# Softmax in a cross-attention kernel: eight exponentials with bias and accumulator on ScalarE in place of one wide exponential and two VectorE passes

## The chip, the cores and the metric

The kernel runs on one core of one Trainium2 chip. The metric is the device time of one execution in microseconds. The profile is that of one further execution of the same program.

## The reference, cut to what matters

Sixteen batches of 1024 tokens, 512 wide, go through a cross-attention over 64 context rows with 8 heads, and then through a mixture of 32 experts (4 per token, 512 places each) with one shared expert beside it. Both parts add to their input.

```python
x = x + xattn(layernorm(x), ctx, Wq, Wk, Wv, Wo, bo)   # q, k, v in 8 heads of 64
    scores = einsum('bhid,bhjd->bhij', q, k) * scale    # 8 heads x 64 columns for each token
    attn = softmax(scores, axis=-1)
    out = einsum('bhij,bhjd->bhid', attn, v)
x = x + ffn(layernorm(x), gate_w, bias, W1, W3, W2, sw1, sw3, sw2)
```

## The kernel before, in words

The program has two parts, one after the other: `set_up_and_tokens` and `experts`. The change lies in the first, which takes some 1440 of the 2031 us of the profile.

The first part takes the tokens in 128 tiles of 128 tokens. A tile passes through many stages, and a loop over steps runs them against each other: step n does the scores of tile n-8 (`SCORES`), the mixing of the values for tile n-9 (`MIX`), the second layernorm and its transposes for tile n-14 (`X2`), and so on. Every fourth step belongs to a group of four tiles, for the shared expert: two steps of each period of four do its upward products (`FFN_UP`, into the banks G_ps and U_ps), the other two the downward ones (`FFN_DOWN`). Below, a tile is named by the number of its scores. Tiles 62, 63, 66 and 67 fall into steps with upward products (tile 62 and 66 the first of the two, 63 and 67 the second), tiles 64 and 65 into steps with downward ones, and so with every other period. In every second period, the step of the last tile (75, for one) also makes keys or values of a later batch (`kv`, evicted by ScalarE into `kbd` or `vbd`); tile 63's and 67's do not.

Each engine has one queue, written out by hand in the order of `step(n)`, and waits with semaphores. No scheduler moves anything. The path of a tile's softmax crosses four engines:

- TensorE (PE): 12 matmuls of the scores into the bank S_ps (L350), and behind them in its queue the mixing of the tile before (L366), gate logits, the transposes of x2 (L376), the shared expert's products, a piece of preparation for the next batch (PREP_ps), and last the four transposes of this tile's probabilities into TP_ps (L477).
- VectorE (DVE): the maximum of each head, into `top_s` (L902); the subtraction of it from S_ps, in place (L915); after the exponential the sums of each head (L934) and their reciprocal `rsum` (L943).
- ScalarE (ACT): one exponential of 128x512 with the layernorm's `rs1` as per-token scale (L576). Ahead of it in the queue stands `x2` (L567), behind it `x2t_h` (L584), in the up steps the `Tanh` of the shared expert (L610, waits for G_ps) and, when VectorE has multiplied it twice (L749, L754), `ht_h` (L613). The next step begins with `pt_h` (L542), the high half of the turned probabilities.
- GpSimd (POOL): the product of the exponentials with `rsum` (L655). Ahead of it in the queue stand `ht_l` (L642, waits for `ht_h`, in the step after an up step), `xt_l` (L649), and four indirect DMAs of the slot table (L631).

The scores of the next tile stand right behind the transposes L477 in TensorE's queue.

## Time and profile before

| what | value |
|---|---|
| median of 3 runs | 2043.02 us (2042.87 to 2050.21) |
| the profiled execution, its own time | 2032.71 us |
| its span in the profile | 2030.9 us |
| TensorE busy | 1805.0 us, 89% |
| VectorE busy | 1511.0 us, 74% |
| ScalarE busy | 736.6 us, 36% |
| GpSimd busy | 1227.6 us, 60% |

The span runs from the first to the last instruction; the 1.8 us around it belong to the execution's own time. The profiled execution was 10.3 us faster than the median. Busy shares are means over both parts of the program, which have different limits, so the stretches have to be read apart.

### The profile page before, as it was taken

What the parts mean: (1) busy time and instruction counts of PE and PEld (TensorE: products, weight loads), DVE (VectorE), ACT (ScalarE), POOL (GpSimd) and SP (SyncE); (2) the same over time, 40 slices, a digit from 0 to 9 for tenths busy, and PEclk for the clock granted to TensorE, in tenths of its full rate; (3) what the DMA queues carried; (4) which work ended last, traced back from release to release, by engine and by line L of the source; (5) the groups of instructions that cost most, each with busy time, mean ns of one, the idle gap of its engine ahead of it and who ended that gap; (6) DMA issues with size and microseconds to landing.
All of it is one profiled execution on the core that took longest, in us unless ns stands there. A gap on an engine that the chain in (4) does not pass through costs nothing. (4 is left out here: it accounts for less than half of the span.)

```text
span 2030.9 us, 31738 instructions
## 1 busy us (share of the span) xinstructions
PE 1805.0 (89%) x9952; PEld 1281.4 (63%) x9952; DVE 1511.0 (74%) x4072; ACT 736.6 (36%) x1252; POOL 1227.6 (60%) x1107
## 2 busy tenths in 40 slices
PE   5789799999999999999999999999750899999992
PEld 4667577777777777777777777776420456555551
DVE  4678688898798889888889888888540477766671
ACT  2233334334434333434333343333210344444440
POOL 1223556666566666566666666666465487888864
PEclk8999899999999999999999999999885899999996
DMA  6123453343233333323323323332214599999986
GB/s 199 54 72 85 79 102 102 95 100 115 88 104 101 96 95 112 94 86 119 96 87 103 113 85 97 105 96 79 67 60 127 148 228 220 231 227 228 228 153 80
DMA packets 194903, 241.43 MB, mean 119 GB/s; under 512 B 59569, under 2 KB 101809, under 8 KB 194738
## 3 DMA queue, kind: packets, MB, share of 16 engines
q1 hardware_dynamic: 149682, 169.89, 28.8%
q0 software_dynamic: 45056, 69.52, 17.3%
q8 instruction: 82, 1.34, 0.3%
q14 instruction: 83, 0.68, 0.1%
HBM read 134.07 MB, written 105.25 MB: 118 GB/s over the span
## 5 line engine op out<-in xcount | busy, mean ns | idle before, releaser
L631 POOL DMA_INDIRECT slot_table<-tok,slot x512 | 504.1, 985 | 128.1 <-issue 122.8
L649 POOL TENSOR_TENSOR xt_l<-xt,xt_h 128x512 fp32r<-128x512 f32 x128 | 165.4, 1293 | 165.8 <-PE S_ps L350 130.3
L1102 POOL DMA_INDIRECT out<-ye,idx x128 | 202.5, 1582 | 89.2 <-issue 35.8
L655 POOL TENSOR_TENSOR prob<-prob,rsum 128x512 f32<-128x512 f32 x128 | 133.8, 1045 | 154.1 <-DVE rsum L943 153.6
L576 ACT ACTIVATE prob<-S_ps,rs 128x512 f32<-128x512 f32 x128 | 88.0, 688 | 364.9 <-DVE S_ps L915 364.9
L1254 DVE TENSOR_TENSOR xe_l<-TE_ps,xe_h 128x512 f16<-128x512 f32 x128 | 88.5, 692 | 177.0 <-issue 90.6
L350 PE MATMUL S_ps<-a_h,xt_h 128*128 128x512 f32 x512 | 214.2, 418 | 1.8 <-DVE m_l L878 1.8
L642 POOL TENSOR_TENSOR ht_l<-hid,ht_h 128x512 fp32r<-128x512 f32 x64 | 83.1, 1298 | 204.7 <-ACT ht_h L613 204.7
L366 PE MATMUL O_ps<-m_h,pt_h 128*128 128x512 f32 x512 | 200.8, 392 | 2.7 <-ACT pt_h L542 2.2
L350 PE MATMUL S_ps<-a_h,xt_l 128*128 128x512 f32 x512 | 202.7, 396 | 0.0
L350 PE MATMUL S_ps<-a_l,xt_h 128*128 128x512 f32 x512 | 201.4, 393 | 0.0
L366 PE MATMUL O_ps<-m_l,pt_h 128*128 128x512 f32 x512 | 199.9, 390 | 0.0
L366 PE MATMUL O_ps<-m_h,pt_l 128*128 128x512 f32 x512 | 199.8, 390 | 0.0
L873 DVE TENSOR_TENSOR pt_l<-TP_ps,pt_h 128x512 fp32r<-128x512 f32 x128 | 88.4, 690 | 118.5 <-ACT pt_h L542 113.3
L1090 POOL DMA_INDIRECT rows<-x2aug,idx x128 | 133.7, 1045 | 43.5 <-issue 38.1
L542 ACT ACTIVATE pt_h<-TP_ps 128x512 fp32r<-128x512 f32 x128 | 75.5, 590 | 204.6 <-PE TP_ps L477 200.5
L1154 PE MATMUL TE_ps<-ident_r,rows 128*128 128x128 f32 x512 | 70.4, 263 | 76.7 <-DMA rows<-x2aug,idx 65.3
L477 PE MATMUL TP_ps<-ident,prob 128*128 128x128 f32 x512 | 81.7, 283 | 50.5 <-POOL prob L655 50.5
L1154 PEld LDWEIGHTS TE_ps<-ident_r,rows 128*128 128x128 f32 x512 | 58.0, 144 | 102.7 <-issue 62.0
L567 ACT ACTIVATE x<-xr,nb,rs 128x512 f32<-128x512 f32 x128 | 104.1, 813 | 42.6 <-DMA x2aug<-x 32.5
L477 PEld LDWEIGHTS TP_ps<-ident,prob 128*128 128x128 f32 x512 | 58.5, 142 | 92.2 <-POOL prob L655 62.1
L366 PEld LDWEIGHTS O_ps<-m_h,pt_h 128*128 128x128 f32 x512 | 96.5, 188 | 26.8 <-issue 2.7
(177 smaller groups left out, 4889.7 us busy)
## 6 DMA issues: line engine op xcount, KB each, us to landing
xt<-in_xT SPq DMA_DIRECT2D x128, 256.0 KB
xr<-in_x SPq DMA_DIRECT2D x32, 1024.0 KB, 6.1
x2aug<-x SPq DMA_DIRECT2D x128, 256.0 KB
out<-xr SPq DMA_DIRECT2D x32, 1024.0 KB
up_w<-in_w SPq DMA_DIRECT2D x64, 256.0 KB
slot_table<-tok,slot POOLq DMA_INDIRECT x512
down_raw<-in_w SPq DMA_DIRECT2D x32, 256.0 KB
x2aug<-wfull SPq DMA_DIRECT2D x32, 64.0 KB
```

Source lines behind the costliest of these rows:

```text
L350: last = pe.matmul(S_ps[:, :], left[:, kc, :], right[:, b % 2, kc, :], start=(m == 0), stop=(m == 3 * KD - 1))
L366: last = pe.matmul(O_ps[:, :], left[:, p * P:(p + 1) * P], right[:, b % 2, p, :], start=(m == 0), stop=(m == 3 * PAIRS - 1))
L477: last = pe.transpose(TP_ps[:, p * P:(p + 1) * P], prob[:, t % 2, 2 * p:2 * p + 2, :].rearrange("p h j -> p (h j)"), ident[:, :])
L567: act.activation(x2[:, :], x_tile(t), ACT.Identity, bias=nb2[:, g % 2, i:i + 1], scale=rs2[:, g % 2, i:i + 1]).then_inc(x2_done, 1)
L631: pool.indirect_dma_start(table, bass.IndirectOffsetOnAxis(ap=slot[:, g % 2, i, q:q + 1], axis=0), tok[:, t:t + 1], None, bounds_check=SLO ...
L649: pool.tensor_tensor(xt_l[:, :, :], xt[:, :, :], xt_h[:, t % 2, :, :].bitcast(F32), ALU.subtract).then_inc(xt_lo, 1)
L655: pool.tensor_tensor(prob[:, t % 2, :, :], prob[:, t % 2, :, :], rsum[:, :].unsqueeze(2).to_broadcast([P, H, SKV]), ALU.mult).then_inc(pro ...
L873: dve.tensor_tensor(pt_l[:, :], TP_ps[:, :], pt_h[:, :].bitcast(F32), ALU.subtract).then_inc(pt_lo, 1)
L1090: pool.indirect_dma_start(rows[:, r, c, :].bitcast(F32), None, x2aug, bass.IndirectOffsetOnAxis(ap=idx[:, e, c:c + 1], axis=0), bounds_che ...
L1102: pool.indirect_dma_start(out, bass.IndirectOffsetOnAxis(ap=idx[:, e, c:c + 1], axis=0), ye[:, e % 4, c, :], None, bounds_check=TOKENS + P ...
L1154: last = pe.transpose(TE_ps[i % 2][:, kc * P:(kc + 1) * P].bitcast(F32R), rows[:, e % RING, i, kc * P:(kc + 1) * P], ident_r[:, :])
L1254: dve.tensor_tensor(xe_l[dst], TE_ps[i % 2][:, :].rearrange("p (c t) -> p c t", c=KD), xe_h[dst], ALU.subtract).then_inc(t_lo, 1)
```

## The change

VectorE no longer subtracts the maximum from the scores and no longer sums the exponentials. It makes a small tile `below` of 128x8 instead, which holds minus the maximum times `rs1`. ScalarE takes the exponential of each head by itself, with that head's column of `below` as bias, `rs1` as scale, and the sum of the head's 64 results written through the accumulator output into `sums`. One signal is given, after the eighth. The wait for `ln1` moves from ScalarE to VectorE; ScalarE gets a wait for `rsum_done` of the tile before, and VectorE one for `exp_done` of the tile before. `below` has two buffers.

```diff
@@ ACT, step(n) @@
                         act.wait_ge(below_done, t + 1)
-                        act.wait_ge(ln1, (g + 1) * NEWTON)
                         after(act, probs_t_done, t - 1)
-                        act.activation(prob[:, t % 2, :, :], S_ps[:, :].rearrange("p (h j) -> p h j", h=H), ACT.Exp,
-                                       scale=rs1[:, g % 2, i:i + 1]).then_inc(exp_done, 1)
+                        after(act, rsum_done, t)
+                        for h in range(H):
+                            last = act.activation(prob[:, t % 2, h, :], S_ps[:, h * SKV:(h + 1) * SKV], ACT.Exp,
+                                                  bias=below[:, t % 2, h:h + 1], scale=rs1[:, g % 2, i:i + 1],
+                                                  accum_out=sums[:, h:h + 1])
+                        last.then_inc(exp_done, 1)
@@ DVE, step(n) @@
                         dve.wait_ge(max_done, s8 + 1)
-                        dve.tensor_tensor(heads, heads, top_s[:, :].unsqueeze(2).to_broadcast([P, H, SKV]),
-                                          ALU.subtract).then_inc(below_done, 1)
+                        dve.wait_ge(ln1, (s8 // 4 + 1) * NEWTON)
+                        after(dve, exp_done, s8 - 1)
+                        dve.tensor_scalar(below[:, s8 % 2, :], top_s[:, :], rs1[:, s8 // 4 % 2, s8 % 4:s8 % 4 + 1], -1.0,
+                                          ALU.mult, ALU.mult).then_inc(below_done, 1)
@@
-                    if s8 is not None:
-                        dve.wait_ge(exp_done, s8 + 1)
-                        dve.tensor_reduce(sums[:, :], prob[:, s8 % 2, :, :], AX.X, ALU.add).then_inc(sum_done, 1)
@@
                     if s8 is not None:
-                        dve.wait_ge(sum_done, s8 + 1)
+                        dve.wait_ge(exp_done, s8 + 1)
                         after(dve, prob_done, s8)
                         dve.reciprocal(rsum[:, :], sums[:, :]).then_inc(rsum_done, 1)
```

On ScalarE, in the last up step of a period without keys and the start of the step after it, the queue reads before (L584 is `x2t_h`, L610 the `Tanh` of G_ps, L613 `ht_h`, L542 the next step's `pt_h`):

```order
L559 ACTIVATE xt_h<-xt 128x512
L567 ACTIVATE x2<-xr,nb2,rs2 128x512
L576 ACTIVATE prob<-S_ps,rs1 128x512
L584 ACTIVATE x2t_h<-TX_ps 128x4x128
L610 ACTIVATE hid<-G_ps 128x512
L613 ACTIVATE ht_h<-hid 128x512
L542 ACTIVATE pt_h<-TP_ps 128x512
```

and now:

```order
L560 ACTIVATE xt_h<-xt 128x512
L568 ACTIVATE x2<-xr,nb2,rs2 128x512
L578 ACTIVATE prob,sums<-S_ps,below,rs1 128x64 x8
L588 ACTIVATE x2t_h<-TX_ps 128x4x128
L614 ACTIVATE hid<-G_ps 128x512
L617 ACTIVATE ht_h<-hid 128x512
L543 ACTIVATE pt_h<-TP_ps 128x512
```

One instruction became eight in the same place; what stands behind it kept its order.

On VectorE, in the step behind that one (tile 64's), from the maximum to the reciprocal, before:

```order
L902 TENSOR_REDUCE top_s<-S_ps 128x8
L915 TENSOR_TENSOR S_ps<-S_ps,top_s 128x512
L930 TENSOR_TENSOR xr<-xr,O_ps 128x512
L934 TENSOR_REDUCE sums<-prob 128x8
L939 BN_STATS st2<-xr 128x6
L943 RECIPROCAL rsum<-sums 128x8
```

and now:

```order
L906 TENSOR_REDUCE top_s<-S_ps 128x8
L921 TENSOR_SCALAR below<-top_s,rs1 128x8
L936 TENSOR_TENSOR xr<-xr,O_ps 128x512
L942 BN_STATS st2<-xr 128x6
L946 RECIPROCAL rsum<-sums 128x8
```

The two passes over 128x512 are gone, and the reciprocal stands right behind L942, waiting for ScalarE.

## Rows read from the trace of the kernel before

**Rows 1.** Busy time by engine in a stretch; then PEclk, DMA share, GB/s

```profile
700.00:1000.00 300.00, 294.65 (x1686) 221.06 (x1685) 260.43 (x780) 118.42 (x206) 192.79 (x181) 1.00 0.33 98
```

**Rows 2.** Waits: engine, line, releaser; us in total, times, longest

```profile
PE TP_ps L477 <- POOL prob L655: 50.5, 39, 9.4
```

**Rows 3.** Groups of ScalarE: count, busy us, mean ns, idle before

```profile
L567 ACT ACTIVATE x<-xr,nb,rs 128x512 f32<-128x512 f32 x128 | 104.1, 813 | 42.6 <-DMA x2aug<-x 32.5 <-issue 7.5 <-DVE nb L727 2.6
L576 ACT ACTIVATE prob<-S_ps,rs 128x512 f32<-128x512 f32 x128 | 88.0, 688 | 364.9 <-DVE S_ps L915 364.9
L559 ACT ACTIVATE xt_h<-xt 128x512 fp32r<-128x512 f32 x128 | 80.9, 632 | 12.4 <-DMA xt<-in_xT 12.4
...
L542 ACT ACTIVATE pt_h<-TP_ps 128x512 fp32r<-128x512 f32 x128 | 75.5, 590 | 204.6 <-PE TP_ps L477 200.5 <-issue 4.1
...
L604 ACT ACTIVATE lexp<-R_ps 128x128 f32<-128x128 f32 x32 | 8.7, 272 | 6.5 <-remote 6.5
```

**Rows 4.** Groups of VectorE, with the same columns

```profile
L915 DVE TENSOR_TENSOR S_ps<-S_ps,top_s 128x512 f32<-128x512 f32 x128 | 87.5, 684 | 1.2
...
L934 DVE TENSOR_REDUCE sums<-prob 128x8 f32<-128x512 f32 x128 | 86.9, 679 | 23.6 <-ACT prob L576 21.8 <-issue 1.8
...
L794 DVE MATCH_VALUE_LOAD taken<-best,biased 128x8 f32 x128 | 10.4, 82 | 0.3 <-DVE best L787 0.3
```

**Rows 5.** Timeline of ScalarE, tiles 62, 63: start, duration, idle before and releaser

```profile
725.80 0.69 ACT L576 ACTIVATE prob<-S_ps,rs 128x512 f32<-128x512 f32 x1 [2.47 <-DVE S_ps L915]
...
728.89 0.60 ACT L610 ACTIVATE hid<-G_ps 128x512 f32<-128x512 f32 x1 [0.75 <-PE G_ps L402]
...
738.22 0.69 ACT L576 ACTIVATE prob<-S_ps,rs 128x512 f32<-128x512 f32 x1 [3.81 <-DVE S_ps L915]
...
739.83 0.60 ACT L610 ACTIVATE hid<-G_ps 128x512 f32<-128x512 f32 x1 [0.43 <-PE G_ps L402]
```

**Rows 6.** The same of ScalarE, tiles 66 and 75 (keys are made beside 75)

```profile
768.74 0.69 ACT L576 ACTIVATE prob<-S_ps,rs 128x512 f32<-128x512 f32 x1 [2.85 <-DVE S_ps L915]
...
771.23 0.60 ACT L610 ACTIVATE hid<-G_ps 128x512 f32<-128x512 f32 x1 [0.80 <-PE G_ps L402]
...
868.02 0.69 ACT L576 ACTIVATE prob<-S_ps,rs 128x512 f32<-128x512 f32 x1 [3.81 <-DVE S_ps L915]
868.61 0.59 ACT L584 ACTIVATE x2t_h<-TX_ps 128x512 f16<-128x512 f32 x1
870.60 1.20 ACT L596 ACTIVATE vbd<-PREP_ps 64x512 f32<-64x512 f32 x2 [1.40 <-PE PREP_ps L439]
872.33 0.60 ACT L610 ACTIVATE hid<-G_ps 128x512 f32<-128x512 f32 x1 [0.53 <-PE G_ps L402]
```

**Rows 7.** Timeline of VectorE: last product of tile 63's step; two of tile 65's

```profile
742.68 0.66 DVE L754 TENSOR_TENSOR hid<-hid,U_ps 128x512 f32<-128x512 f32 x1
...
758.39 0.67 DVE L915 TENSOR_TENSOR S_ps<-S_ps,top_s 128x512 f32<-128x512 f32 x1
...
761.24 0.18 DVE L943 RECIPROCAL rsum<-sums 128x8 f32<-128x8 f32 x1
```

**Rows 8.** Timeline of GpSimd: tile 61's product; then tile 64's step

```profile
718.57 1.04 POOL L655 TENSOR_TENSOR prob<-prob,rsum 128x512 f32<-128x512 f32 x1 [1.52 <-DVE rsum L943]
...
744.09 1.30 POOL L642 TENSOR_TENSOR ht_l<-hid,ht_h 128x512 fp32r<-128x512 f32 x1 [2.46 <-ACT ht_h L613]
...
751.60 1.06 POOL L655 TENSOR_TENSOR prob<-prob,rsum 128x512 f32<-128x512 f32 x1
```

**Rows 9.** Timeline of TensorE: transposes of tiles 61, 64, 65 and 66

```profile
720.33 0.66 PE L477 MATMUL TP_ps<-ident,prob 128*128 128x128 f32 x4
...
752.72 0.66 PE L477 MATMUL TP_ps<-ident,prob 128*128 128x128 f32 x4 [0.97 <-POOL prob L655]
...
762.60 0.66 PE L477 MATMUL TP_ps<-ident,prob 128*128 128x128 f32 x4
...
773.64 0.60 PE L477 MATMUL TP_ps<-ident,prob 128*128 128x128 f32 x4
```

More of the change, by code:

```diff
@@ L150, in set_up_and_tokens @@
         top_s = sb("top_s", [P, H], F32)
+        below = sb("below", [P, 2, H], F32)
         sums = sb("sums", [P, H], F32)
@@ L216, in set_up_and_tokens @@
         x2_t_done, logits_done = sem("x2_t_done"), sem("logits_done")
-        max_done, below_done, sum_done, rsum_done = sem("max_done"), sem("below_done"), sem("sum_done"), sem("rsum_done")
+        max_done, below_done, rsum_done = sem("max_done"), sem("below_done"), sem("rsum_done")
         exp_done, pt_hi, x2_done, x2t_hi = sem("exp_done"), sem("pt_hi"), sem("x2_done"), sem("x2t_hi")
```

## The prediction

> **What bounds the kernel now.** I read first the busy times by stretch, because the two parts of the program differ. In the middle of the part with tokens TensorE is busy 294.7 us of 300, at the full clock (1.00, so 2.4 GHz), VectorE 260.4, ScalarE only 118.4 [rows 1]. TensorE's queue sets the pace, and any wait that reaches it is paid in full. Next the waits: TensorE stood 50.5 us, 39 times, before the transposes of the probabilities, for GpSimd's product with the reciprocal [rows 2]. The end of the softmax path is thus already what TensorE waits for. Last the timelines, for who makes it late. For tile 64 the wait is 0.97 us [rows 9]; the product there started at 751.60 without idle time in front [rows 8], so GpSimd's own queue was the limit: from `ht_l` at 744.09 to this product are 7.51 us of queued work, and `ht_l` had waited for `ht_h` [rows 8], which waits for VectorE's last product at 742.68 [rows 7], which goes back to the Tanh of tile 63 at 739.83 [rows 5]. For tile 65 there is next to no spare: the reciprocal began at 761.24 [rows 7], and the transposes at 762.60 [rows 9]. VectorE and ScalarE have idle time on average, which is worth nothing unless it lies on one of these two paths.
>
> **What goes.** Per tile VectorE loses the subtraction, 684 ns, and the sums, 679 ns [rows 4], and gains `below`, 128x8, which I price as the reciprocal of the same shape, 0.18 us [rows 7]: 1.18 us less, 151 us of busy time over 128 tiles. Little of it shortens the path, since the reciprocal now waits for ScalarE.
>
> **What comes, E.** I call E the time from the start of the first of eight exponentials to the end of the eighth. One exponential of 512 columns is 688 ns now. A copy of 512 columns from PSUM takes 590, an exponential of 128 columns with a fixed scale 272, so a column costs (590-272)/384 = 0.83 ns and 64 columns 272-53 = 219 ns. Two operands read per partition (bias and scale) cost 813-632 = 181 ns more. That makes 400 ns for one head [rows 3]. Neighbours on ScalarE overlap by 0.1 us: tile 75's exponential takes 0.69 us from 868.02, and `x2t_h` begins at 868.61 [rows 6]. So 0.30 us apart, and E = 8 x 0.30 + 0.10 = 2.5 us if the accumulator's output is free. No row shows an accumulator output. The nearest is VectorE's match, one call in the program that leaves an extra row of 82 ns [rows 4]; on ScalarE the fixed part of the shortest ACTIVATE, 272-106 = 166 ns [rows 3], is what a second, tiny instruction per head could take. Overlapped it adds 0.07 and E is 3.1; not overlapped it adds 0.17 and E is 3.8; if it also takes away the overlap of its neighbours, 8 x 0.566 = 4.5. I take the middle, 3.4, and keep 2.5 and 4.5 as ends. E below 2.5 would need deeper overlap than these rows have.
>
> The page "ScalarE: Activation LUTs" of the Trainium skill (section "What ACT_TABLE_LOAD costs") gives 280 ns + 0.833 ns per column with a pointer bias, 93 ns for each further pointer and an overlap of 93 ns. By it E would be 8 x 0.333 + 0.09 = 2.8 without the accumulator, and the sum below about +25 us. The trace agrees on the pointer (688 against 590 ns, [rows 3]). The page's budget of 0.3 us per ACTIVATE speaks against splitting one into eight. "VectorE: DVE Perf Modes" (section "Two Vector instructions with no wait between them") says that on VectorE an accumulator output is a second instruction; no row here shows it for ScalarE.
>
> **The softmax path itself.** Before, the subtraction began 2.85 us ahead of the reciprocal in tile 65 (758.39, 761.24) [rows 7]. Now: `below` 0.17 + hand-over 0.05 + E + hand-over 0.04 = E + 0.26 (the hand-overs are estimates from starts and ends of neighbouring engines' rows). With E = 3.4 that is 3.66: +0.81 us. Tile 65 has nothing to spare, so TensorE pays 0.8. Tile 61, the same place in another period, ends its product at 718.57 + 1.04 = 719.61, and TensorE comes at 720.33 [rows 8, 9]: it pays 0.14. Half the 32 periods are of each kind: 16 x 0.81 + 16 x 0.14 = 15 us. Tile 66, in an up step, pays nothing: its exponentials end at 771.64 (below), and with 0.04 and the 1.36 us from reciprocal to transposes (761.24 to 762.60) its probabilities are ready at 773.04, before TensorE comes at 773.64 [rows 9].
>
> **What is queued behind the exponentials.** In the up steps the Tanh stands behind `x2t_h`, and in the first of them also behind `lexp`. The exponential starts 0.5 us earlier than now (0.22 behind the start of the small operation, against 0.67 + 0.05 behind the subtraction's). Tile 66: 768.24, end 771.64, Tanh 0.56 later at 772.20 instead of 771.23, +0.97. Tile 62: 725.30, end 728.70, Tanh 729.26 instead of 728.89, +0.38 [rows 5, 6]. From there it goes through both VectorE products, `ht_h`, `pt_h`, to the next maximum, all one after the other: the next tile starts that much later, less where TensorE's own delay covers it. Tile 63 (with tile 66's or tile 62's delay, by kind): exponentials 737.72 to 741.12, Tanh 0.39 later at 741.51 instead of 739.83, +1.68, and with the delay carried in +2.65 or +2.06. GpSimd cannot start `ht_l` before that has passed, and its 7.51 us follow unchanged. The reciprocal of tile 64 arrives another 0.18 us later than this queue. TensorE, which had waited 0.97 already, pays it all: 2.83 or 2.24, mean 2.53. In it lies what tile 63's own transposes lose. In periods with keys ScalarE first has to wait 1.40 us for the keys and 0.53 for G_ps [rows 6]; tile 75's exponentials run 867.52 to 870.92, the eviction follows at 871.31 instead of 870.60 and the Tanh at 872.5: +0.2, with the carried delay and the 0.18 from 0.7 to 1.3, mean 1.0. Sum: 16 x 2.53 + 16 x 1.0 = 56 us.
>
> **The sum.** 15 + 56 = 71 us in the part with tokens; the part with experts has none of these instructions. On the profiled execution 2032.7 + 71 = 2104 us; the median of runs lies 10 us higher, so 2043 + 71 = 2114 us, +3.5%. By the same steps E = 2.5 gives +13 us, 3.1 +41, 3.8 +124, and 4.5 +221: above 3 each 0.1 us of E costs about 10 us or more, since delays pass from one step to the next.
>
> **Rivals.** (a) *The accumulator is free*, E = 2.5: 2056 us. For it: the program has one instruction per head. Against it: 8 results must be written somewhere. (b) *Each head is fully serial*, E = 4.5: 2264 us. For it: a read of the accumulator has to wait for its ACTIVATE. Against: the 0.1 us overlap everywhere else. (c) *Faster*: the short ACTIVATEs overlap far more than wide ones, down to E = 1.7 or less; then the Tanh of tile 63 still waits only for G_ps (738.22-0.5+1.7+0.39 = 739.81, [rows 5]), no queue behind is late, and VectorE's lighter load of memory accesses lets GpSimd's six operations ahead of tile 64's product run 0.1 us shorter each: 32 x 0.6 = 19 us less, 2024 us. It decides below E = 1.7, against 400 ns each from [rows 3]. (d) *VectorE's relief cancels the cost*: its 1.18 us per tile would pull the maxima forward. Against it: VectorE waits at the start of most steps for `pt_h` anyway. It would give 2035 to 2050.
>
> **Chances.** Forecast with E from 2.8 to 4.1: 60%. (a) 14%, (b) 15%, (c) 4%, (d) 7%. The range takes in (a) and most of (b): 2050 to 2230 us. A measurement of this kernel tells about 0.5% (10 us) from no change: faster 5%, same 9%, slower 86%.
>
> **What would show it.** In the changed profile: E itself, from eight rows of ScalarE, and whether rows of an accumulator's read stand between; VectorE's busy time down by about 150 us, with new idle time before the reciprocal, released by ScalarE; the idle time of ScalarE before Tanh gone in up steps; TensorE's wait for GpSimd before L477 grown from 50 to about 120 us; the distance `ht_l` to product in tile 64 still 7.5 us. I am wrong if E is under 2 or over 4.5, if TensorE's clock falls with its waits, or if tile 64's product starts from VectorE's reciprocal long after its own queue was free.

## The result, and the profile after

| | before | after |
|---|---|---|
| median | 2044.8 us (2042.87 to 2050.21, 4 runs) | 2146.55 us (2140.51 to 2154.34, 4 runs) |
| profiled execution, its own time | 2032.71 us | 2154.34 us |
| span | 2030.9 us | 2152.6 us |

The kernel is slower: ratio 1.0501 [1.0469, 1.0532], +102 us, where 71 had been forecast. The two profiled executions lie further apart, 121.7 us, since that of before was 12 us under its median and that of after 8 us over its own. The busy times of the page, first the whole program after (engine, us, share, instructions), then its costliest groups of the softmax path:

```profile
PE 1852.4 (86%) x9952; PEld 1306.2 (61%) x9952; DVE 1438.8 (67%) x3944; ACT 1043.5 (48%) x3172; POOL 1226.1 (57%) x1107
...
L578 ACT ACTIVATE prob<-S_ps,below,rs 128x64 f32<-128x64 f32 x1024 | 398.0, 409 | 376.3 <-DVE below L921 373.2
...
L578 ACT ACTIVATION_READ_ACCUMULATOR prob<-S_ps,below,rs 128x1 f32 x1024 | 214.6, 210 | 0.0
...
L946 DVE RECIPROCAL rsum<-sums 128x8 f32<-128x8 f32 x128 | 25.9, 203 | 208.9 <-ACT prob L578 208.1
```

VectorE is busy 72 us less (1511.0 to 1438.8) although two passes of 87.5 and 86.9 us are gone [rows 4], ScalarE 307 us more. There is an instruction that the kernel does not write out: behind each of the 1024 exponentials stands a read of the accumulator, 210 ns by itself. The reciprocal now stands idle for ScalarE for 208 us.

Most of the time is in the middle of the tokens' part. A stretch from the first score matmul of tile 20 to that of tile 124, 104 tiles, of before and then of after (columns as in [rows 1]):

```profile
257.60:1397.80 1140.20, 1115.35 (x6376) 834.55 (x6375) 979.51 (x2931) 447.52 (x776) 720.31 (x676) 1.00 0.34 99
```

```profile
275.80:1512.10 1236.30, 1151.41 (x6377) 850.17 (x6375) 924.72 (x2827) 696.61 (x2336) 718.42 (x676) 0.98 0.32 91
```

104 tiles take 96.1 us longer; of the rest of the 121.7 us, 18.2 lie ahead of this stretch (it begins at 275.80 instead of 257.60) and 7.4 behind it. TensorE's idle time in the stretch went from 24.9 to 84.9 us (length less busy time), and its busy time rose by 36 us for the same matmuls: the granted clock is 0.98 instead of 1.00. So there are two losses, waits and a slower clock. The waits, and the answers to [rows 1] and [rows 2]:

```profile
700.00:1000.00 300.00, 281.43 (x1554) 206.95 (x1552) 222.26 (x686) 170.15 (x571) 173.50 (x164) 0.98 0.32 93
```

```profile
PE TP_ps L478 <- POOL prob L659: 112.8, 69, 12.9
...
ACT hid L614 <- PE G_ps L403: 6.6, 7, 2.6
```

TensorE waits 112.8 us for GpSimd's product (50.5 before). The idle time of ScalarE before the Tanh, for TensorE's G_ps, is nearly gone: 6.6 us in the whole program, 39.8 before.

**Tile 64 of the kernel after**, engine by engine. ScalarE, which answers to [rows 5, 6] (start, duration; idle time before and its releaser):

```profile
797.40 0.62 ACT L588 ACTIVATE x2t_h<-TX_ps 128x512 f16<-128x512 f32 x1
797.87 0.63 ACT L614 ACTIVATE hid<-G_ps 128x512 f32<-128x512 f32 x1
...
806.84 0.40 ACT L578 ACTIVATE prob<-S_ps,below,rs 128x64 f32<-128x64 f32 x1 [2.98 <-DVE below L921]
807.15 0.19 ACT L578 ACTIVATION_READ_ACCUMULATOR prob<-S_ps,below,rs 128x1 f32 x1
807.24 0.39 ACT L578 ACTIVATE prob<-S_ps,below,rs 128x64 f32<-128x64 f32 x1
...
809.82 0.22 ACT L578 ACTIVATION_READ_ACCUMULATOR prob<-S_ps,below,rs 128x1 f32 x1
```

The first two rows are of tile 63's step: the Tanh stands right behind `x2t_h`, without idle time. The others give E = 809.82 + 0.22 - 806.84 = 3.20 us. An exponential takes 0.40, its read starts 0.09 before its end, and the next exponential 0.09 behind the start of the read: 0.38 us per head by (809.53 - 806.84)/7.

VectorE, tiles 63 and 64, which answers to [rows 7]:

```profile
794.07 0.23 DVE L921 TENSOR_SCALAR below<-top_s,rs 128x8 f32<-128x8 f32 x1
...
804.78 0.68 DVE L906 TENSOR_REDUCE top_s<-S_ps 128x8 f32<-128x512 f32 x1
805.50 1.31 DVE L921 TENSOR_SCALAR below<-top_s,rs 128x8 f32<-128x8 f32 x1
...
810.07 0.20 DVE L946 RECIPROCAL rsum<-sums 128x8 f32<-128x8 f32 x1 [1.95 <-ACT prob L578]
```

The same operation on 128x8 numbers takes 0.23 us in one tile and 1.31 in the next. It is so in nearly every period: in 25 of the 26 tiles of tile 64's place in the stretch it takes over 0.7 us, with a mean of 1.28 over the 26, and in the other three places at most 0.32. GpSimd in the same step, which answers to [rows 8]:

```profile
801.75 1.28 POOL L646 TENSOR_TENSOR ht_l<-hid,ht_h 128x512 fp32r<-128x512 f32 x1 [2.85 <-ACT ht_h L617]
...
805.47 1.30 POOL L653 TENSOR_TENSOR xt_l<-xt,xt_h 128x512 fp32r<-128x512 f32 x1
...
810.36 1.04 POOL L659 TENSOR_TENSOR prob<-prob,rsum 128x512 f32<-128x512 f32 x1 [1.16 <-DVE rsum L946]
```

`xt_l` started 0.03 us before `below` and ended at 806.77; `below` ended at 806.81. The product waited 1.16 us for the reciprocal: its own queue was free at 809.20, 7.45 us behind `ht_l`, nearly the 7.51 of before.

TensorE, which answers to [rows 9]:

```profile
811.46 0.72 PE L478 MATMUL TP_ps<-ident,prob 128*128 128x128 f32 x4 [2.05 <-POOL prob L659]
...
812.40 0.63 PE L351 MATMUL S_ps<-a_l,xt_h 128*128 128x512 f32 x1
...
816.07 0.39 PE L351 MATMUL S_ps<-a_h,xt_l 128*128 128x512 f32 x1
```

and the granted clock in three stretches of scores, tiles 64, 65 and 66 (the column before the DMA share):

```profile
799.30:802.40 3.10, 3.05 (x15) 2.21 (x13) 2.18 (x12) 1.36 (x3) 0.66 (x1) 1.00 0.69 247
811.80:816.10 4.30, 4.30 (x15) 3.44 (x14) 3.06 (x9) 2.30 (x4) 1.72 (x2) 0.60 0.01 0
824.10:827.20 3.10, 3.10 (x17) 2.51 (x16) 3.07 (x10) 2.42 (x4) 1.67 (x2) 1.00 0.11 36
```

TensorE had stood idle 2.05 us; in the stretch behind it the clock is 0.60 on average, which is 1.2 GHz for most of it, and a score matmul takes 0.63 us instead of 0.39. From the start of the first of a tile's 12 score matmuls to the start of the last are 2.6 us at full clock. It took over 3 us in 16 of the 104 tiles, always behind a tile of tile 64's place in its period; before, in one. I call these slow scores.

### The profile page after: what moved, and what is told of

It reads as the page before. It is cut to its first block and busy times, and to the rows that moved or that the text cites. A ratio compares the mean times of both kernels' runs of the same rounds, so it can differ in the third digit from the quotient of the medians.

```text
span 2152.6 us, 33657 instructions
## 1 busy us (share of the span) xinstructions
PE 1852.4 (86%) x9952; PEld 1306.2 (61%) x9952; DVE 1438.8 (67%) x3944; ACT 1043.5 (48%) x3172; POOL 1226.1 (57%) x1107
## 5 line engine op out<-in xcount | busy, mean ns | idle before, releaser
L578 ACT ACTIVATE prob<-S_ps,below,rs 128x64 f32<-128x64 f32 x1024 | 398.0, 409 | 376.3 <-DVE below L921 373.2
L351 PE MATMUL S_ps<-a_h,xt_h 128*128 128x512 f32 x512 | 226.8, 443 | 1.8 <-DVE m_l L882 1.8
L578 ACT ACTIVATION_READ_ACCUMULATOR prob<-S_ps,below,rs 128x1 f32 x1024 | 214.6, 210 | 0.0
L351 PE MATMUL S_ps<-a_l,xt_h 128*128 128x512 f32 x512 | 213.3, 417 | 0.0
L351 PE MATMUL S_ps<-a_h,xt_l 128*128 128x512 f32 x512 | 212.7, 415 | 0.0
L478 PE MATMUL TP_ps<-ident,prob 128*128 128x128 f32 x512 | 85.3, 291 | 112.8 <-POOL prob L659 112.8
L946 DVE RECIPROCAL rsum<-sums 128x8 f32<-128x8 f32 x128 | 25.9, 203 | 208.9 <-ACT prob L578 208.1
```

What stands on the lines that cost most here:

```text
L351: last = pe.matmul(S_ps[:, :], left[:, kc, :], right[:, b % 2, kc, :], start=(m == 0), stop=(m == 3 * KD - 1))
L478: last = pe.transpose(TP_ps[:, p * P:(p + 1) * P], prob[:, t % 2, 2 * p:2 * p + 2, :].rearrange("p h j -> p (h j)"), ident[:, :])
L578: last = act.activation(prob[:, t % 2, h, :], S_ps[:, h * SKV:(h + 1) * SKV], ACT.Exp, bias=below[:, t % 2, h:h + 1], scale=rs1[:, g % 2, ...
```

## Steps per place in the period

For the experiments I use one table, worked out from the starts of the first score matmul of each tile, tiles 20 to 123: the mean time from one tile to the next, in us, by the place in the period of four. "64" is tile 64's place, and so on. The last columns are the 104 tiles together and how many of them had slow scores.

```
kernel     "64"   "65"   "66"   "63"   104 tiles  slow scores
before     10.44  10.33  10.90  12.17  1140.2     1
after      12.30  11.57  10.95  12.73  1236.3    16
x_warm     12.25  10.72  10.93  12.70  1211.7     0
x_pos      11.92  10.33  10.94  12.20  1180.1     2
x_port     10.87  10.17  10.92  12.17  1147.1     0
x_read     12.28  11.67  10.91  12.84  1240.4    10
x_read2    12.07  10.90  11.38  12.71  1223.7     4
x_queue    11.22  10.33  10.97  12.26  1164.3     0
x_split    11.18  10.91  10.93  12.59  1185.7     1
x_same     10.41  10.31  10.98  12.18  1140.8     1
x_pool2     9.61  10.59  10.92  12.17  1125.6     0
x_onemax   10.49  10.16  10.90  12.14  1136.0     0
x_best      9.69  10.22  11.05  12.15  1120.8     0
```

A slow set of scores lengthens the step of the place "65" (11.57 in after, 10.72 where the clock holds). Single long steps are in the means too: in the profiles of before, x_same, x_onemax and x_best TensorE stood idle for 11 to 20 us between 200 and 310 us for ScalarE's `x2`, which waited for a DMA. They fall ahead of tile 20 or behind it, and 5 us there are 0.2 us in a mean of 26. The ratios below are each against the kernel before on the same chip; its median there was 2036.0 us (x_warm, x_pos, x_port, x_read), 2019.9 (x_queue, x_split, x_pool, x_best) and 2037.2 us (x_read2, x_same, x_pool2, x_onemax), so ratios, and not times, are compared.

## Experiments on the place and the neighbour of `below`

My theory after the trace: the eight exponentials cost what was forecast, and the surplus comes from `below`, which waits for GpSimd, and from the clock. The rival: ScalarE's longer work alone makes all of it.

**x_pos.** `below` right behind the maximum, instead of behind three chains of other work.

```diff
                         dve.tensor_reduce(top_s[:, :], heads, AX.X, ALU.max).then_inc(max_done, 1)
+                        dve.wait_ge(max_done, s8 + 1)
+                        dve.wait_ge(ln1, (s8 // 4 + 1) * NEWTON)
+                        after(dve, exp_done, s8 - 1)
+                        dve.tensor_scalar(below[:, s8 % 2, :], top_s[:, :], rs1[...], -1.0,
+                                          ALU.mult, ALU.mult).then_inc(below_done, 1)
                     chain(n, 2, 3)
...
                     chain(n, 3, 4)
-                    (the same lines, from here)
```

> The changed kernel, with VectorE's small operation that makes the bias placed directly behind the maximum, ahead of the statistics and Newton steps that stood between. It still runs on VectorE from SBUF operands. Theory: in tiles 62, 63, 65, 66 the exponentials start 0.6 to 1.6 us earlier, the Tanh of tile 63 with them, and tile 65's transposes no longer wait; in tile 64, where the operation stood right behind the maximum already, it keeps its 1.3 us (0.23 elsewhere), which it spends beside GpSimd's xt_l and so is a wait for GpSimd. Time 2080 to 2100 us. Rival (the place does not matter, since ScalarE is late by itself): above 2135.

Measured: 2089.16 us, ratio 1.0253 [1.0198, 1.0308]. Half of the loss is gone with the eight exponentials, the reads and E = 3.2 us untouched. In tile 65's place the cost is gone entirely (10.33). In tile 64's place it is not. VectorE of x_pos, tile 64, and its group over the whole program:

```profile
772.63 1.31 DVE L910 TENSOR_SCALAR below<-top_s,rs 128x8 f32<-128x8 f32 x1
```

```profile
L910 DVE TENSOR_SCALAR below<-top_s,rs 128x8 f32<-128x8 f32 x128 | 116.0, 906 | 4.5
```

Beside it, GpSimd of x_pos:

```profile
772.61 1.30 POOL L653 TENSOR_TENSOR xt_l<-xt,xt_h 128x512 fp32r<-128x512 f32 x1
```

Again it starts within 0.02 us of `xt_l` and ends with it. The mean of `below` rose to 906 ns from 485 in the kernel after, since at the new place it meets GpSimd's work in more tiles; the steps of the other places are at most 0.04 us longer than before. What `below` had stood behind was partly such a wait itself: in tile 63 of the kernel after, a Newton step of 1.69 us, shown further below.

**x_port.** The bias by ScalarE itself: the maximum is negated in its reduction, and a ninth, small ACTIVATE multiplies it by `rs1`. VectorE's small operation is gone, all else is as after.

```diff
-                        dve.tensor_reduce(top_s[:, :], heads, AX.X, ALU.max).then_inc(max_done, 1)
+                        after(dve, below_done, s8)
+                        dve.tensor_reduce(top_s[:, :], heads, AX.X, ALU.max, negate=True).then_inc(max_done, 1)
...
+                        act.wait_ge(max_done, t + 1)
+                        act.wait_ge(ln1, (g + 1) * NEWTON)
+                        act.activation(below[:, t % 2, :], top_s[:, :], ACT.Identity,
+                                       scale=rs1[:, g % 2, i:i + 1]).then_inc(below_done, 1)
                         act.wait_ge(below_done, t + 1)
...
-                        (VectorE's tensor_scalar into below, with its waits)
```

> The changed kernel, with the bias made by ScalarE itself (one ACTIVATE of 128x8 with rs1 as scale, on a maximum that VectorE's reduction already negates); VectorE's small operation is gone. It differs from x_pos by the engine. Theory (in tile 64 VectorE's small operation waited 1.1 us for GpSimd): exponentials of tile 64 start 1.0 us earlier than in x_pos, TensorE's idle time there falls under 1 us and the clock does not drop in tile 65: 2050 to 2075 us. Rival (the 1.3 us of the small operation is work and not a wait): within 10 us of x_pos, since ScalarE gives 0.3 us for it.

Measured: 2048.87 us, ratio 1.0066 [1.0046, 1.0087], 1 us under the range's lower end. ScalarE and GpSimd of x_port, tile 64:

```profile
767.40 0.30 ACT L576 ACTIVATE below<-top_s,rs 128x8 f32<-128x8 f32 x1 [1.24 <-issue]
767.73 0.40 ACT L582 ACTIVATE prob<-S_ps,below,rs 128x64 f32<-128x64 f32 x1
```

```profile
767.39 1.29 POOL L657 TENSOR_TENSOR xt_l<-xt,xt_h 128x512 fp32r<-128x512 f32 x1
```

The small operation starts 0.01 us behind the same GpSimd instruction and takes 0.30 us. So GpSimd's work delays it on VectorE and not on ScalarE. Between x_pos and x_port the 104 tiles differ by 33.0 us; 26 tiles of tile 64's place by 1.31 - 0.30 = 1.0 us are 26, and the two slow sets of scores of x_pos are some 4 more. E is 3.21 us here too: ScalarE does all that it does in the change and one ACTIVATE more, and the kernel costs 0.7%. The rival falls.

The page "SBUF — State Buffer" of the Trainium skill (section "SBUF: two separate sides") says that VectorE, in its faster modes or with two inputs in this memory, and GpSimd share a pair of ports to it, that whichever starts first holds it for its whole instruction, and that ScalarE has its own. The trace agrees for `below` in tile 64, though which mode VectorE was in no row tells: it ended 0.04 us behind `xt_l`, which had started first. On who starts first other rows do not bear the page out: the Newton step of 1.69 us began 0.36 us ahead of `xt_l`, and still ended 0.04 behind it; a DMA of the slot table stood on GpSimd until just before, but beside such a DMA alone the same step took 0.15 us (1391.19 in the kernel before). VectorE's pass over PSUM was not delayed. The subtraction, at the same place in the kernel before, took 684 ns on average over 128 [rows 4], and in tile 64 it ran beside the same GpSimd instruction:

```profile
747.84 1.30 POOL L649 TENSOR_TENSOR xt_l<-xt,xt_h 128x512 fp32r<-128x512 f32 x1
747.85 0.70 DVE L915 TENSOR_TENSOR S_ps<-S_ps,top_s 128x512 f32<-128x512 f32 x1
```

## Experiment on the clock

**x_warm.** The kernel after, with eight matmuls that nobody reads put ahead of the wait for the probabilities in tile 64's place of each period. They fill TensorE's idle time there and change nothing else.

```diff
-                    pe.wait_ge(prob_done, t + 1)
...
+                    if t % 4 == 0 and t >= 8:
+                        for k in range(8):
+                            pe.matmul(TP_ps[:, :], ones[:, :], up_sb[:, 0, :], start=True, stop=True)
+                    pe.wait_ge(prob_done, t + 1)
```

> The changed kernel, with eight matmuls of 128x512 that nobody reads, written into TP_ps ahead of TensorE's wait for the probabilities in every fourth step (tiles 64, 68, ...), from tile 8 on. They take about 1.8 of the 2.05 us in which TensorE stands idle there. Theory (the idle time of tile 64 lets the granted clock fall, and the scores of tile 65 then run at half rate: 4.0 instead of 2.6 us in the changed kernel's trace): the scores of tile 65 take 2.6 us again, PEclk 1.00 in the middle stretch, and some 17 to 21 drops of 1.5 us each go: 2113 to 2123 us. Rival (the slow scores have another cause, such as reads of memory beside them): unchanged at 2146 or slower.

Measured: 2122.24 us, ratio 1.0423 [1.0383, 1.0463]. No tile has slow scores, and the 104 tiles take 1211.7 us instead of 1236.3, at a granted clock of 1.00:

```profile
270.80:1482.50 1211.70, 1167.84 (x6560) 851.83 (x6584) 921.32 (x2833) 697.34 (x2336) 719.16 (x676) 1.00 0.32 93
```

Nearly all of the 24.6 us lies in the place "65" (11.57 to 10.72, 26 x 0.85 = 22 us); the steps of tile 64's place, with their wait for the probabilities, stayed as long (12.30 and 12.25). So the clock cost about 25 us in the stretch, beside the idle time ahead of it, and the remaining +71.5 us are waits.

## Experiments on the exponentials and the accumulator

**x_read.** The kernel after without `accum_out`: VectorE sums again, with the second layernorm's statistics between sums and reciprocal.

```diff
-                                                  bias=below[...], scale=rs1[...], accum_out=sums[:, h:h + 1])
+                                                  bias=below[...], scale=rs1[...])
...
+                        dve.tensor_reduce(sums[:, :], prob[:, s8 % 2, :, :], AX.X, ALU.add).then_inc(sum_done, 1)
                         (bn_stats of the tile before)
+                        dve.wait_ge(sum_done, s8 + 1)
                         dve.reciprocal(rsum[:, :], sums[:, :]).then_inc(rsum_done, 1)
```

> The changed kernel, with the exponentials written without the accumulator output and the sums made by VectorE again (one pass of 128x512, 0.68 us, behind the eighth exponential). Everything else as changed. Theory (what is queued behind the exponentials on ScalarE carries the cost): the read of the accumulator, 0.09 us apart per head in the changed kernel, goes, E falls from 3.2 to 2.5 us, and the Tanh in up steps comes 0.7 us earlier; the softmax path itself stays about as long (0.75 us less, 0.65 us more for the sums). Time 2105 to 2125 us, from 2146. Rival (only the length of the softmax path counts): path within 0.1 us, time unchanged, 2140 to 2150.

Measured: 2156.9 us, ratio 1.0594 [1.0553, 1.0636]. I had expected less time than after, and it took more. E fell to 2.47 us, as it should, but the path from there to the reciprocal grew:

```profile
809.50 0.69 DVE L939 TENSOR_REDUCE sums<-prob 128x8 f32<-128x512 f32 x1 [1.95 <-ACT prob L578]
810.11 0.68 DVE L944 BATCH_NORM_STATS2 st<-xr 128x6 f32<-128x512 f32 x1
810.71 0.19 DVE L948 RECIPROCAL rsum<-sums 128x8 f32<-128x8 f32 x1
```

The reciprocal starts 1.21 us behind the first of them, not 0.6: the statistics stood in its way. From the first exponential to the reciprocal are 2.47 + 0.04 + 1.21 = 3.72 us, and 3.24 in the kernel after. I had counted the sums and not what was queued behind them.

**x_read2.** The same with the reciprocal right behind the sums.

```diff
                         dve.tensor_reduce(sums[:, :], prob[:, s8 % 2, :, :], AX.X, ALU.add).then_inc(sum_done, 1)
+                        dve.wait_ge(sum_done, s8 + 1)
+                        dve.reciprocal(rsum[:, :], sums[:, :]).then_inc(rsum_done, 1)
                         (bn_stats of the tile before)
-                        (the reciprocal, from here)
```

> x_read with VectorE's reciprocal directly behind the sums, ahead of the statistics of the second layernorm, which in x_read stood between and cost 0.6 us on the softmax path. So the softmax path is as long as in the changed kernel (0.73 us less of exponentials, 0.65 more of sums) and ScalarE's queue 0.73 us shorter. Theory (x_read was slow because of that order): ratio to the kernel before between 1.035 and 1.050, under the changed kernel's. Rival (the pass over prob costs more than its 0.65 us, through other operations that it pushes back): 1.055 or more, as x_read.

Measured: 2130.81 us, ratio 1.0449 [1.0409, 1.0489], as expected. From the end of the exponentials to the reciprocal are 0.75 us, and E is 2.48: together 3.23, as much as the 3.20 and 0.04 of the kernel after. So the accumulator is even on the path: eight reads add (3.20 - 2.48) = 0.72 us, 0.09 each, and save one pass of 0.7 us. What it wins beside that is VectorE's time, and in one place TensorE waits for it: in 24 of the 26 tiles of the place "66" the step of x_read2 takes some 0.3 us more. In tile 66 of both kernels VectorE goes without idle time into `pt_l`, the low half of the turned probabilities, which the mixing needs, and there it ends 0.33 us later in x_read2. (The interval of x_read2 overlaps that of the kernel after, [1.0469, 1.0532], it has 12 sets of slow scores fewer, and I don't read a gain into the difference.)

**x_split.** The kernel before, with its exponential as eight of 64 columns, the fixed `rs1` scale, no bias and no accumulator; subtraction and sums stay.

```diff
-                        act.activation(prob[:, t % 2, :, :], S_ps[:, :].rearrange(...), ACT.Exp, scale=rs1[...]).then_inc(exp_done, 1)
+                        for h in range(H):
+                            last = act.activation(prob[:, t % 2, h, :], S_ps[:, h * SKV:(h + 1) * SKV], ACT.Exp, scale=rs1[...])
+                        last.then_inc(exp_done, 1)
```

> The kernel before, with its exponential of 128x512 split by heads into eight of 128x64, with neither bias nor accumulator output; VectorE subtracts and sums as before. The cost of eight instructions alone: E = 8 x 0.21 + 0.1 = 1.8 us instead of 0.69. Theory (path and queue both get 1.1 us longer): tile 65 pays 1.1 or 0.4 us, tile 64 0.3 to 0.8 us: 30 to 50 us over the kernel before. Rival (GpSimd's queue covers it): under 10 us.

Measured: 2073.65 us, ratio 1.0264 [1.0229, 1.03], +53.8 us, a little over the range. Its group on ScalarE, and a row of its timeline:

```profile
L577 ACT ACTIVATE prob<-S_ps,rs 128x64 f32<-128x64 f32 x1024 | 223.9, 330 | 378.0 <-DVE S_ps L917 378.0
```

```profile
792.72 1.55 ACT L577 ACTIVATE prob<-S_ps,rs 128x64 f32<-128x64 f32 x7 [2.37 <-DVE S_ps L917]
```

In tile 64 seven of them stand in one row of 1.55 us: (1.55 - 0.33)/6 = 0.20 us apart though each takes 0.33. E is 1.75, 1.06 longer than one wide one. That alone costs 45 us in the 104 tiles, spread over the places "64", "65" and "63": one microsecond more of E, with everything else as before, costs nearly half of what the whole change does (96.1). By itself the split is dearer than x_port, which splits too but leaves out the subtraction and the sums.

**x_queue.** The kernel before, with 14 small copies that nobody reads behind the exponential in ScalarE's queue. They don't touch the softmax path, only what stands behind it.

```diff
                                        scale=rs1[:, g % 2, i:i + 1]).then_inc(exp_done, 1)
+                        for k in range(14):
+                            act.activation(idle[:, k, :], wo_sb[:, k % PAIRS, 0:64], ACT.Copy)
```

> The kernel before, with fourteen small copies of 128x64 on ScalarE behind the one wide exponential, to a tile that nobody reads: about 2.1 us more in ScalarE's queue, nothing more on the softmax path. Theory (ScalarE's queue carries part of the cost by itself, through the Tanh of tile 63, ht_h and the late start of tile 64): Tanh of tile 63 about 1.5 us later, half of the periods pay 1.5 us, the others 0.3: 25 to 35 us over the kernel before, and up to 55 if the longer idle time of TensorE lets its clock fall. Rival (only the softmax path and the late bias count): 0 to 8 us over the kernel before.

Measured: 2046.39 us, ratio 1.0131 [1.011, 1.0153], +26.5 us, as expected. ScalarE of x_queue, tile 64, and the group:

```profile
768.82 0.69 ACT L577 ACTIVATE prob<-S_ps,rs 128x512 f32<-128x512 f32 x1 [2.37 <-DVE S_ps L918]
769.40 2.14 ACT L580 ACTIVATE idle<-wo_sb 128x64 bf16<-128x64 f32 x14
771.45 0.57 ACT L587 ACTIVATE x2t_h<-TX_ps 128x512 f16<-128x512 f32 x1
```

and GpSimd in the same step:

```profile
764.33 1.28 POOL L645 TENSOR_TENSOR ht_l<-hid,ht_h 128x512 fp32r<-128x512 f32 x1 [3.53 <-ACT ht_h L616]
...
771.80 1.06 POOL L658 TENSOR_TENSOR prob<-prob,rsum 128x512 f32<-128x512 f32 x1
```

The place "64" grows by 0.8 us, where the forecast saw it: Tanh late, `ht_h` late, GpSimd's queue late. The product again starts without idle time in front, 7.47 us behind `ht_l`, and on average over the 26 tiles `ht_l` stands 0.85 us later in the step than before, and the product 0.79. The other places hardly change. So the second term of the forecast exists apart from the first.

## Experiments on the kernel before: what the path was waiting for

If GpSimd's queue is the limit in tile 64, an order that shortens it should gain, and the repeat of before should show how far two builds differ.

**x_same.** The kernel before, unchanged.

> The kernel before, unchanged, profiled beside the three others of this job, so that their stretches can be compared on one chip: the middle of the part with tokens (tiles 20 to 124), the stretch of tiles 16 to 20, the gap between the two parts, and the part with experts. The ratio to the kernel before is 1.000 within its interval, and the middle stretch takes 1140 us.

Measured: 2038.08 us, ratio 0.9999 [0.9984, 1.0015]; 104 tiles in 1140.8 us (1140.2 in the profile of before).

**x_pool** and **x_pool2**, one kernel measured twice: the last two DMAs of the slot table behind GpSimd's product instead of ahead of it.

```diff
-                    file(at(n, TABLE), 2, TOP)
                     (the product with rsum)
+                    file(at(n, TABLE), 2, TOP)
```

> The kernel before, with the last two of a step's four slot-table DMAs put behind the product with the reciprocal in GpSimd's queue, instead of ahead of it. Theory (in tile 64 the product waits for GpSimd's own queue, not for the reciprocal): it starts 0.8 us earlier there, TensorE's idle time before L477 falls from 50 to about 20 us: 15 to 28 us under the kernel before. Rival (the reciprocal is what comes last): no change, within 5 us.

> x_pool once more, beside the profile of the kernel before on the same chip. In x_pool's trace the middle stretch (tiles 20 to 124) was only 1 us shorter than before's: tile 64 gained 0.8 us, but the bias-free subtraction of tiles 61 and 65 came 0.7 us later. Theory (the gain of 18 us lies outside the middle stretch): ratio 0.985 to 0.995 again, with the middle stretch at 1139 us and the difference in the first 20 tiles or the gap between the parts. Rival (the first measurement was drift): ratio 0.998 or more.

Measured: 2002.03 us, ratio 0.9907 [0.9886, 0.9928], and 2024.11 us, ratio 0.9928 [0.9903, 0.9954]. The ratio came as expected both times, but I had expected the second profile to show its gain outside the 104 tiles, and that was wrong: they take 1125.6 us, 15.2 less than in x_same. The first profile (1139.3 us) had hidden it behind two long steps, of tiles 20 and 24, which took 13 us more than the others of their place. TensorE waited there 4.1 and 6.1 us for ScalarE's `x2`, and that for a DMA (ScalarE stood idle 6.53 and 8.68 us for it); why the DMA was late I did not find. GpSimd in tile 64 of x_pool2:

```profile
749.08 1.04 POOL L654 TENSOR_TENSOR prob<-prob,rsum 128x512 f32<-128x512 f32 x1 [1.60 <-DVE rsum L943]
```

The product now waits 1.60 us for VectorE and starts 0.8 us earlier in the step than before. The two DMAs had taken 2.5 us of the queue ahead of it (749.14 to 751.60 in the kernel before); only 0.8 came off, since VectorE's path was right behind. The place "65" pays back 0.3 us of the 0.8 (10.31 to 10.59).

**x_onemax.** The change with one maximum for the whole row instead of one per head: one bias of 128x1 by ScalarE, one wide exponential, sums on VectorE with the reciprocal right behind. The softmax is the same with any shift common to a head's columns; a head whose scores lie far below the largest of the row would lose digits, and no run here shows how far apart heads can lie before that matters.

```diff
-                        dve.tensor_reduce(top_s[:, :], heads, AX.X, ALU.max).then_inc(max_done, 1)
+                        dve.tensor_reduce(top_s[:, 0:1], S_ps[:, :], AX.X, ALU.max, negate=True).then_inc(max_done, 1)
...
-                        dve.tensor_tensor(heads, heads, top_s[...].to_broadcast([P, H, SKV]), ALU.subtract)
...
+                        act.activation(below[:, t % 2:t % 2 + 1], top_s[:, 0:1], ACT.Identity, scale=rs1[...])
-                        act.activation(prob[...], S_ps[...], ACT.Exp, scale=rs1[...])
+                        act.activation(prob[...], S_ps[...], ACT.Exp, bias=below[:, t % 2:t % 2 + 1], scale=rs1[...])
```

> x_best with GpSimd's order as in the kernel before: one maximum over 512 columns, bias made by ScalarE, one exponential of 128x512 with it, reciprocal right behind the sums. Theory (in tile 64 the product waits for GpSimd's queue, so a shorter softmax path gains nothing there by itself): ratio 0.993 to 1.000, with the middle stretch 0 to 8 us shorter, and the wait of 0.9 us in tile 64 still there. Rival (the path decides): 0.983 as x_best.

Measured: 2022.24 us, ratio 0.9916 [0.9886, 0.9946], slightly better than expected. The 104 tiles take only 4.2 us less than before; in tile 64 the product still stands behind the DMAs (it starts at the same 6.0 us behind the scores, though the reciprocal is there at 4.1). Another 10 us (against x_same) were won in the first 16 tiles, which I had not expected and did not take apart.

**x_best.** Both together.

> The kernel before with three edits: one maximum over all 512 columns of a token instead of one per head (softmax is the same for any shift), negated by the reduction; bias of 128x1 made by ScalarE; one exponential of 128x512 with that bias, so that VectorE's subtraction goes and its sums stay, with the reciprocal right behind them; and GpSimd's order of x_pool. Theory: softmax path about 1 us shorter than before in every step, ScalarE's queue 0.4 us longer, no wait of TensorE left before L477: 25 to 35 us under the kernel before. Rival (TensorE's own work bounds it already): within 8 us.

Measured: 1987.0 us, ratio 0.9833 [0.9813, 0.9854], 33 us faster than before, as expected, and about the sum of what each brings alone (0.9928 and 0.9916). ScalarE and GpSimd in tile 64, then the waits and a stretch as in [rows 1]:

```profile
746.36 0.29 ACT L576 ACTIVATE below<-top_s,rs 128x1 f32<-128x1 f32 x1 [1.41 <-DVE top_s L907]
746.69 0.78 ACT L580 ACTIVATE prob<-S_ps,below,rs 128x512 f32<-128x512 f32 x1
```

```profile
748.73 1.04 POOL L658 TENSOR_TENSOR prob<-prob,rsum 128x512 f32<-128x512 f32 x1 [1.08 <-DVE rsum L940]
```

```profile
PE TP_ps L478 <- POOL prob L658: 24.5, 12, 9.8
```

```profile
700.00:1000.00 300.00, 299.84 (x1717) 225.09 (x1716) 258.74 (x767) 133.18 (x239) 194.20 (x183) 1.00 0.35 102
```

The bias costs the wide exponential 0.78 - 0.69 = 0.09 us and its own small operation 0.3; eight exponentials with their reads made 0.69 into 3.20. TensorE is busy 299.84 of 300 us, so there is hardly more to win from the softmax path in this stretch.

## Why the prediction was right, and where it was wrong

The sign and the range held, and so did the chain that the forecast saw: the reciprocal waits for ScalarE, and TensorE for the product. The size was 71 forecast and 102 measured. Two of the prediction's own signs of being wrong came true beside that: TensorE's clock fell, and tile 64's product started from VectorE's reciprocal 1.16 us after its own queue was free. Step by step:

- **E**, forecast 3.4 us between 2.5 and 4.5: 3.20. The read of the accumulator exists, and is overlapped, at 0.09 us a head; that is 0.02 more than the overlapped case of 0.07. The spacing without it came out at 0.29, where 0.30 was forecast.
- **Tile 65**, forecast +0.81 with E = 3.4, which is +0.61 with 3.20: the transposes (823.70 in the kernel after) came at 7.24 us behind the end of the scores instead of 6.49, +0.75. From the start of `below` to that of the first exponential, priced at 0.22, were 0.34. Right in kind, 0.13 us short. Over both kinds the mean forecast was 0.48 a period, and 10.72 - 10.33 = 0.39 came where the clock is out of play (x_warm).
- **Tanh and GpSimd's queue**, in tile 64: 7.51 us from `ht_l` to the product forecast, and the queue took 7.45. The shape was right, and x_queue shows the term by itself.
- **The reciprocal arrives another 0.18 us later than this queue**: this is the term that failed. It arrived 1.16 us behind it. Its working priced `below` at 0.17 us, from the reciprocal of the same shape, and in tile 64 it took 1.31, since it started beside `xt_l`. The price was right for tile 63 (0.23) and wrong for the tile that decides. x_pos kept the wait at another place, x_port took it away by giving the operation to ScalarE, and 33 us of the 104 tiles went with it. In periods without keys the steps of the places "63" and "64" grew by 1.01 us (10.93 to 11.94) and 1.96 (10.66 to 12.62), 2.97 together against 2.53 forecast. In periods with keys the forecast was 1.0, and 0.03 (13.61 to 13.64) and 1.82 (10.13 to 11.95) came, 1.85 together. These are means over the 13 and the 12 periods of the stretch.
- **The clock**: named as something that would make me wrong, with no term in the sum. It fell behind 16 of 26 tiles of tile 64's place and cost about 25 us of the 104 tiles' 1236. With waits of 2 us forecast in one place of every period, it should have been a case with a chance and a price.
- **VectorE's relief**, forecast 150 us: 72. The two passes went (174 us), and `below` took 62.1 us instead of 22:

```profile
L921 DVE TENSOR_SCALAR below<-top_s,rs 128x8 f32<-128x8 f32 x128 | 62.1, 485 | 1.2
```

  By these groups that is 112 us less, and 105 by the lengths of all of VectorE's rows. The page counts 72 less, since neighbouring rows overlap in a full queue and it counts the overlap once: a pass that goes takes away less than its own length. I had added lengths.

  The wait of `below` could have been seen in the trace of before. Its nearest row was not the reciprocal but a Newton step of 128x4 numbers in SBUF, in the kernel before and then in one tile of the kernel after, beside GpSimd's `xt_l` from 792.59 to 793.88:

```profile
L696 DVE TENSOR_SCALAR rs<-nt 128x4 int32<-128x4 int32 x64 | 64.8, 1013 | 0.0
```

```profile
792.23 1.69 DVE L700 TENSOR_SCALAR rs<-nt 128x4 int32<-128x4 int32 x1
```

  A mean of 1013 ns for four columns, where its neighbour of the same size and kind takes 160, is a sign that something else holds it. In the kernel before, 58 of its 64 instances run beside an `xt_l`: they take 0.53 to 1.92 us and end 0.03 to 0.04 behind it. The other six, the one at 515.38 for instance, take 0.15 to 0.17.
- **TensorE's wait for GpSimd**, forecast about 120 us: 112.8. That it came so near is partly luck, as below.

The forecast was closer than its parts deserve. By its own slope E = 3.2 gives +51 us, not 71, so the E that was too long covered part of what was missing. Against the 104 tiles (0.81 of the 128): 41 us by the forecast's steps with the true E; the port wait adds 26 x 1.08 = 28; that makes 69, and x_warm has +71.5; the clock adds 24.6, and after has +96.1. The 41 is worked out and not measured: no run has the eight exponentials with `below` late and undelayed. The runs themselves, each against the next in the 104 tiles, take off 24.6 us for the clock (x_warm), 31.6 for the place of `below` (x_pos), 33.0 for its engine (x_port), and leave 6.9 for eight exponentials with their reads and an early, undelayed bias. So the slope of the forecast, 10 us for each 0.1 us of E, holds at most where the bias comes late; that the sum came near with E too long and `below` too short is partly luck.

**Rivals.** (a), a free accumulator, and (b), serial heads, fall with E = 3.20; the reads are there and overlapped. (c) needed E under 1.7; even with one operand and no accumulator it is 1.75, in x_split, and slower; and GpSimd's queue ahead of tile 64's product got 0.06 us shorter (7.51 to 7.45), where that rival had priced 0.6. (d), VectorE's relief cancels the cost, came near to truth under other conditions: x_port has the relief, the same E, an early bias, and lands at +0.7%.

**Open.** Why the clock fell behind some of TensorE's waits in tile 64's place and not behind others of the same length. In the kernel after 23 of the 26 waits were of 2.0 us or more (all but one of them 2.03 to 2.08), and it fell behind 16 of these; behind the three of 1.0 to 1.7 us it did not. In x_pos 12 of the 26 were of 1.6 or 1.7 us, and 14 of 2.0 or more, of which only two brought slow scores. Tile 64's own in x_pos did not:

```profile
778.60 0.66 PE L478 MATMUL TP_ps<-ident,prob 128*128 128x128 f32 x4 [2.06 <-POOL prob L659]
...
779.32 0.39 PE L351 MATMUL S_ps<-a_l,xt_h 128*128 128x512 f32 x1
```

What differs is the tile before: in the kernel after TensorE also stood idle about 0.8 us in tile 63, and in x_pos it did not. That goes some way and not all of it. Of the long waits of the kernel after, 11 of the 13 with such idle time in the tile before brought slow scores, and 5 of the 10 without; in x_read2 13 waits of 2.01 to 2.07 us stood behind an idle time of 0.6 to 0.9, and only 4 brought them. No run varied it alone. Nor was it tried to fill VectorE's queue so that `below` misses `xt_l` with its place unchanged.

## What to carry to other kernels

A wide ScalarE instruction split to use its bias and accumulator takes some 0.3 us per piece of 64 columns (eight took 2.47 us, the wide one 0.69), and the accumulator about 0.1 more; count it on the path, where the eight reads are even with one VectorE pass, and not in busy time. A tiny VectorE operation on SBUF that stands on the critical path should be priced by the GpSimd instruction that may run beside it, or be given to ScalarE; and its place in the queue counts as much (31.6 us for the place, 33.0 for the engine). Where a change is forecast to make TensorE wait some 2 us at a time, put a clock term into the sum. Before optimising an engine ask what stands in the queue ahead of the last step of the path: two moved DMAs with one shared maximum were worth 1.7%, the change as made cost 5%.

## What the hardware showed that I had not expected

- An accumulator output on ScalarE is a second instruction, ACTIVATION_READ_ACCUMULATOR, in the records 210 ns long on average; the next ACTIVATE starts 0.09 us behind its start. 0.38 us per head with it, 0.29 without ((2.47 - 0.41)/7 in x_read, whose ACTIVATEs take 0.41).
- A VectorE operation on 128x8 numbers in SBUF took 1.31 us instead of 0.23 beside a GpSimd operation of 1.30 us, and ended 0.04 us behind it; on ScalarE, beside the same instruction, it took 0.30. A 128x4 one in the kernel before took 0.15 us alone and up to 1.92 beside it.
- Two operands per partition instead of one cost 0.08 us an ACTIVATE of 64 columns (409 against 330 ns), and the spacing grew by 0.09 (0.29 against 0.20).
- TensorE's clock fell to its lower level (0.63 us a score matmul instead of 0.39) behind an idle time of 2.05 us in one kernel, and stayed at full speed behind one of 2.06 us in another; in the kernel after it fell behind 16 of the 23 waits of 2.0 us or more in tile 64's place.
